# z loads of tiles 4 to 16 that wait for TensorE's turn of the tile four before, in an attention and mixture-of-experts block

## What is computed

```python
x = x + xattn(layernorm(x), ctx, ctx, mask, ...)   # relu(q Wq + bq), relu(k Wk + bk), relu(v Wv + bv);
                                                   # relu(q k') / sqrt(512) + mask, times v, relu
x = x + ffn(layernorm(x), gate_w, Wu, Wv, Wo)

def ffn(x):                                        # E = 8 experts, R = 128, K = 2
    logits = x @ gate_w                            # (tokens, 8)
    topv, topi = top_k(logits, 2); w = softmax(topv)
    s = silu(x @ Wu[e]) * (x @ Wv[e])              # for every expert e
    Y = s @ Wo[e]
    return sum over the two chosen e of w * Y[e]
```

## Time and profile before

| | before |
|---|---|
| runs, us | 418.5, 416.92, 417.95 (median 417.95) |
| span of the profiled execution, us | 432.6 |
| time of the profiled execution outside its span | not recorded beside the three runs |
| PE, DVE, ACT, POOL busy | 94%, 77%, 63%, 49% |
| chain that ended last: PE, DVE, ACT | 67%, 12%, 7% |
| DMA, mean | 203 GB/s, 87.66 MB |

### The profile page before, as it was taken

How to read it: one execution, slowest core, us unless ns; L and a number is a source line. 1 busy time by engine, 2 the same in 40 slices (tenths; PEclk the granted TensorE clock), 3 DMA queues, 4 the chain that set the end, 5 groups by cost and what they waited for, 6 DMA issues and landing times.

```text
span 432.6 us, 10243 instructions
## 1 busy us (share of the span) xinstructions
PE 405.4 (94%) x3031; PEld 360.0 (83%) x3031; DVE 332.0 (77%) x1108; ACT 274.5 (63%) x596; POOL 213.7 (49%) x227
## 2 busy tenths in 40 slices
PE   8999999999999999999979679999999999999990
PEld 6688898899898989987768659888899999999970
DVE  2669998999999999989636568887888666666650
ACT  1786988888888888877635446666666444444430
POOL 2011134666666666662465543333333367878882
PEclk9999999999999999999989699999999999999996
DMA  8823335766667765533883337949975799998793
GB/s 291 259 73 97 123 117 195 248 225 228 221 233 250 248 225 195 188 152 85 295 298 121 123 131 228 361 134 309 309 238 190 214 225 268 273 293 141 105 107 89
DMA packets 49557, 87.66 MB, mean 203 GB/s; under 512 B 7648, under 2 KB 18400, under 8 KB 49376
## 3 DMA queue, kind: packets, MB, share of 16 engines
q1 hardware_dynamic: 35600, 52.37, 38.0%
q0 software_dynamic: 13904, 34.62, 27.9%
HBM read 44.77 MB, written 48.29 MB: 215 GB/s over the span
## 4 chain that ended last, share of the span: by engine, by line
PE 67%; DVE 12%; ACT 7%; issue 4%; another core or an unknown queue 4%; DMA 2%; POOL 2%; SPq 1%; POOLq 0%; DVEq 0%; ACTq 0%
PE psQ L1511 12%; PE psQ L1509 12%; PE psQ L1510 11%; PE psT L1505 10%; PE psO L1509 2%; PE psO L1510 2%; PE psO L1511 2%; DVE qT L941 2%; PE psZ L1509 2%; PE psZ L1510 2%; PE psZ L1511 2%; PE psQ L1505 2%; PE psS L1509 2%; PE psG L1605 2%
## 5 line engine op out<-in xcount | busy, mean ns | idle before, releaser
L941 DVE TENSOR_TENSOR qT<-psT,qT 128x512 fp32r<-128x512 f32 x103 | 69.5, 688 | 33.4 <-ACT qT L744 24.8
L1509 PE MATMUL psQ<-wuv,qT 128*128 x284 | 87.5, 308 | 0.9 <-issue 0.5
L630 POOL DMA_INDIRECT z_dram<-zb x64 | 71.5, 1117 | 32.1 <-DVE zb L1229 15.7
L1510 PE MATMUL psQ<-wuv,qT 128*128 x284 | 81.4, 286 | 0.0
L1511 PE MATMUL psQ<-wuv,qT 128*128 x284 | 81.2, 286 | 0.0
L1509 PE MATMUL psQ<-qT,wq 128*128 128x256 f32 x256 | 75.4, 295 | 2.1 <-DVE qT L941 2.1
L1511 PE MATMUL psQ<-qT,wq 128*128 128x256 f32 x256 | 72.4, 283 | 0.0
L1510 PE MATMUL psQ<-qT,wq 128*128 128x256 f32 x256 | 72.3, 283 | 0.0
L744 ACT ACTIVATE qT<-psT 128x512 fp32r<-128x512 f32 x103 | 59.4, 594 | 17.6 <-PE psT L1505 12.3
L1509 PEld LDWEIGHTS psQ<-wuv,qT 128*128 128x128 f32 x284 | 54.7, 193 | 5.4 <-issue 1.6
L812 ACT ACTIVATE gate_work<-psQ 128x128 f32<-128x128 f32 x71 | 19.7, 277 | 61.3 <-PE psQ L1511 45.3
(11 more groups left out here) (305 smaller groups left out, 1068.3 us busy)
## 6 DMA issues: line engine op xcount, KB each, us to landing
wq_flat<-z_dram SPq DMA_DIRECT2D x28, 264.0 KB
xin<-in_x_dram SPq DMA_DIRECT2D x11, 512.0 KB, 3.6
z_dram<-spare SPq DMA_DIRECT2D x17, 264.0 KB
qpT_flat<-z_dram SPq DMA_DIRECT2D x11, 264.0 KB
zT_ctxT<-in_x_dram SPq DMA_DIRECT2D x5, 512.0 KB, 3.5
kpT_flat<-z_dram SPq DMA_DIRECT2D x9, 264.0 KB
vp_flat<-z_dram SPq DMA_DIRECT2D x9, 264.0 KB
xn<-z_dram SPq DMA_DIRECT2D x8, 264.0 KB
```

Of the source, the lines that this page charges most:

```text
L630: pool.indirect_dma_start(out=z_dram, out_offset=bass.IndirectOffsetOnAxis(ap=z_of(b)[:, t, ROW_COL + k:ROW_COL + k + 1].bitcast(U32), axi ...
L941: nc.vector.tensor_tensor(o, a, b, ALU.subtract).then_inc(s, 1)
L1509: pe.matmul(o, w[LO], a[HI], start=first, stop=False)
L1510: pe.matmul(o, w[HI], a[LO], start=False, stop=False)
```

## The change

A constant AHEAD = 4 is added, and in `load_z` a wait: for tiles 4 to 16 SP waits until PE has counted g_turned up to t - 3, which is when the turn of tile t - 4 is done.

```diff
@@ -58,6 +58,7 @@
 LISTS = 3 * E
 PAD = 16
 RING = 20
+AHEAD = 4
 
 
 
@@ -527,6 +528,8 @@
                     sp.wait_ge(o_done, 2 * NB)
                 if t == 18:
                     sp.wait_ge(stage_lo, 3 * E)
+                if AHEAD <= t < EARLY:
+                    sp.wait_ge(g_turned, t - AHEAD + 1)
                 q = t % RING
                 if t >= RING:
                     sp.wait_ge(res_stored[q], landed(t - RING))
```

## The result

The changed kernel takes 422.12 us (median of 4 runs, 420.26 to 424.95), the kernel before 417.44 us (4 runs, 415.73 to 418.5): a ratio of 1.0125, 95% interval 1.0091 to 1.0159, so 5.2 us slower by the ratio (0.0125 x 417.44) and 4.7 by the medians. The forecast was 421.8, a loss of 3.8 on a median of 417.95. Three executions of all that follow, of 558.26 us (experiment 5), 787.14 us (experiment 12) and 998.58 us (the kernel before), ran in another, slow state, and no median or ratio here counts them.

What follows compares the result with a forecast made beforehand. PE (TensorE), busy 94% of the span, was taken to bound the kernel. Load 17's shift of 5.0 us less a margin of 1.2 gave a 3.8 us loss, added to 417.95 for 421.8 us; range 417.5 to 426.0.

Steps and rivals of the forecast that it cites:

- Loads 4 to 15 cost nothing, load 16 everything: SP's z loads: waits of 4 and 5 cost nothing; 6 to 16 land with 5 us to spare, costing nothing themselves.
- What is queued behind the wait is the cost: SP's in-order queue: the tail-row list, schedule check and load 17 now stand behind load 16, which waits for tile 12.
- The shift of load 17, 5.0 us: On SP after tile 12's turn: 1.15 + 9.3 + 0.80 us puts load 17 at 267.16 instead of 262.15 us.
- The margin of 1.2 us: Tiles 17 to 21: slack between a load's landing and its turn, taken off the 5.0, leaving a 3.8 us loss.
- Load 25 absorbs the shift: Load 25 on SP already waits 8.2 us for the schedule's third part, so it absorbs 5.0 us.
- A microsecond lost before 290 us is lost for good, and none is added later: PE is full after 290 us (busy 69.77 of 70), so the 3.8 us loss is added to the median unchanged.
- (1) Quick loads: Loads 17 to 21 land faster, margin 3 us or more: no measurable change, 419.7 us; chance 0.16 of rival 1's 0.24.
- (2) Faster: At 219 to 226 us, spreading the load burst ends waits with POOL's scatters, returning 8.3 us: 413.4 us; chance 0.08.
- (3) Half clock: After PE's stalls at tiles 17 to 21, a lower clock costs 2.8 us more; chance 0.13 together with (4).
- (4): Loads 6 to 16 are themselves late because the wait is too short: 420 to 430 us; chance 0.02, counted with (3).

Runs made afterwards that it cites:

- experiment 5: Changed kernel with AHEAD = 3 instead of 4; 424.76 us, ratio 1.021 to the kernel before.
- experiment 12: Changed kernel with AHEAD = 5, and POOL's first return of a put-aside tile stored three tiles later; 419.87 us, ratio 1.0081.
- experiment 1: The kernel before, no edit, run again for a second profile, the base for shift and loss; 416.08 us, a single run.
- experiment 4: Changed kernel with the tail-row list, the copies and the wait for head_stored moved behind load 24, thirteen waits kept; 423.98 us, ratio 1.016.
- 3: loads 4 to 10: Changed kernel with only loads 4 to 10 waiting for their turns, 11 to 16 free; 417.07 us, ratio 1.0003.
- 9: the kernel before, later return: The kernel before, with POOL's first return of a put-aside tile stored behind tile 50 instead of 47; 417.46 us, ratio 1.0009.
- 6: AHEAD = 6: Changed kernel with AHEAD = 6 instead of 4; 417.06 us, ratio 1.0013.
- 8: half the list: Changed kernel with all waits, but four experts' tails not read and their four copies at fixed addresses; 418.37 us, ratio 1.0034.
- 7: eight more register loads: The kernel before, without the change's waits, with eight more register loads of tail_i behind the sixteen; 421.15 us, ratio 1.0111.
- 11: the same, later return: The kernel before with eight more register loads behind the list, and POOL's first return stored behind tile 50; 420.38 us, ratio 1.0072.
- 2: load 16 alone: Changed kernel with only load 16 waiting, loads 4 to 15 running ahead as before; 422.41 us, ratio 1.0114.
- experiment 10: Changed kernel with POOL's first return of a put-aside tile stored behind tile 50; 421.6 us, ratio 1.0108.

## Why the prediction held

Shift and loss of the kernels, from the rows described in experiment 1 (us; the loss of experiment 4, at tile 25, lies behind these turns):

| kernel | shift of load 17 | loss, turn 16 to 22 | shift less loss |
|---|---|---|---|
| 4: list moved behind load 24 | -0.1 | 0.0 | |
| 3: loads 4 to 10 | 0.0 | 0.2 | |
| 9: the kernel before, later return | 0.0 | 0.2 | |
| 6: AHEAD = 6 | 1.5 | 0.2 | |
| 8: half the list | 1.5 | 0.3 | |
| 12: AHEAD = 5 | 3.8 | 1.9 | 1.9 |
| 7: eight more register loads | 3.9 | 2.3 | 1.6 |
| 11: the same, later return | 4.0 | 3.5 | 0.5 |
| 2: load 16 alone | 6.3 | 4.4 | 1.9 |
| 10: the change, later return | 6.2 | 4.1 | 2.1 |
| the change | 6.3 | 5.7 | 0.6 |
| 5: AHEAD = 3 | 8.6 | 7.2 | 1.4 |

- **Loads 4 to 15 cost nothing, load 16 everything.** Right: experiments 3 and 2.
- **What is queued behind the wait is the cost.** Right: the list of register loads is no longer covered. Without half of it the stall is gone (8), with eight more it appears with no wait at all (7).
- **The shift of load 17, 5.0 us.** This is the mis-sized term: it measured 6.3. Load 17 was to come 1.15 + 9.3 + 0.80 = 11.25 us behind the turn of tile 12, and comes 12.98 behind it. The list is 1.3 of the difference, 10.58 us or 0.66 each, since I took the pace of its first six loads (0.58 us), not that of all sixteen (0.73). The measured one lies between. In the kernel before, the distance was 6.65 (experiment 1) and not 6.2, which takes 0.4 back. That the 6.2 came so near is in part luck. I counted it from ACT's start at 255.91, but PE's own row has this turn done at 252.77, in the disturbed part of that profile:

```profile
252.17 0.60 PE L1505 MATMUL psT<-ident,kpT_flat 128*128 128x128 f32 x4
```

  From there the distance would have been 9.4 and the shift 1.9 (no view tells when the signal reached SP). In experiment 1 ACT starts 0.04 us behind the turn and the two ways agree.
- **The margin of 1.2 us.** Right within its spread: in the seven kernels that lose time, shift less loss is 0.5 to 2.1, 1.4 in the mean. By landing events of experiment 1, the smallest margin of tiles 17 to 21 was 1.8 us, at tile 21 and not at tile 19, where the sum had it: it gave every load one flight of 4.45 us, and load 21 took 5.0 there.
- **Load 25 absorbs the shift.** PE does not wait at tile 25, so the effect is right, but the way is not: SP's wait before load 25 gave 0.8 us and not 5.0. In experiment 1 it was 7.6 us, the longest of this row, and after it was 6.8:

```profile
SPq L511 <- DVE sched_exp L1098: 8.5, 2, 7.6
```

  The third part of the schedule came later together with PE, written at 269.38 in experiment 1 and at 275.91 in the changed kernel, and load 25 behind it. In experiment 10 PE waits 0.3 us at tile 25 although SP still waited 6.6 us for the schedule.
- **A microsecond lost before 290 us is lost for good, and none is added later.** The first half is right. The second is what I missed: a lag behind the last turn that is 1.9 us longer in the profile of the change. The sum for that profile is 0.8 us that it is late before tile 16 already (as it is at tile 0, so not by the change), 5.7 of loss, 0.4 to 0.5 up to tile 70, and 1.9 of lag: 8.8, the difference of the spans. The mean loss of the three profiles with a shift of 6.2 to 6.3 is 4.7, and the times differ by 4.7 (medians) or 5.2 (ratio). How much the lag makes in an average run is not settled; without its longer form in either kernel the difference is 4.1 (experiments 9 and 10).

So the mechanism held, and the number is nearer than its terms: 421.8 against 422.12 rests on a shift 1.3 us too small, on a base of 417.95 where the median with one more run is 417.44, and on a lag that the sum did not have.

The rivals. (1) Quick loads: some flights are indeed short, 2.6 us for load 17 of the changed kernel, by its landing. The 2.6 us that the Trainium skill's page DMA: Bandwidth & Descriptors, section "Anatomy of one DMA — SWDGE (gpsimd) path", gives by estimate is met there, and nearly by load 17 in experiments 2, 6 to 8 and 10 to 12 (2.7 to 2.8), but by none of loads 18 to 21 in the changed kernel, which take 3.7 to 6.1: load 21 takes 6.11, and the smallest margin decides, so rival 1 fails. (2) Faster: fell with experiments 1 and 3. (3) Half clock: not in the profile of the changed kernel. But experiment 10, which has the same waits on SP, shows it behind a wait of 1.83 us before tile 17 (columns as in the earlier trace rows):

```profile
255.00:258.50 3.50, 3.50 (x17) 3.15 (x16) 2.10 (x6) 1.45 (x3) 0.37 (x1) 0.51 0.94 327
```

It cost little there, as PE would have waited for tile 18's load instead, which landed at 258.26 and was turned at 258.40. In experiments 4 and 5 it stands behind single waits of 5.3 and 4.6 us. (4) did not happen.

## What to carry to other kernels

A wait put into an in-order queue costs what stands behind it and was covered until now, in this case sixteen register loads that used to run while the queue waited for something else; look for the last thing on the queue that had slack, and ask what it did in that slack. Price a serial list by its whole length and not by its first entries. And look at the end of the kernel too: in some profiles SP's aside stores, each of which waits for the one before, slipped by some 4 us more than PE did, and POOL had no slack behind them. They did so with and without a stall of PE, so one profile cannot say that the change is the cause.

## What the runs showed that I had not expected

- The span of a single profile was 14.65 us longer than the median of the runs, with waits that no record names; a second profile of the same kernel, with a span of 414.4 us in a run of 416.08, had none.
- One wait of 4.6 us before tile 17 was followed by a window with a granted clock of 0.52, that is near 1.2 GHz, for 7 us (experiment 5). In the changed kernel four waits of 0.59 to 1.80 us, some 5.2 us in sum within 17 us, were followed by none, but in experiment 10 a single one of 1.83 us was followed by 3.5 us at 0.51. So the length of the longest wait did not decide it alone.
- Loads of the same 264 KB landed 2.6 to 6.1 us after their issue within twelve microseconds of one profile (loads 17 and 21 of the changed kernel), so a margin worked out from one duration is known to a microsecond or two and not better.
